# Shared-expert blocks 12 to 15 load turned operands from memory, and the freed tile becomes two more result buffers

## The reference

```python
x = x + 0.5 * ffn(layernorm(x))      # called "a" below
x = x + mamba(layernorm(x))          # "m"; adds its own input as a residual too
x = x + 0.5 * ffn(layernorm(x))      # "b"

def ffn(flat):                       # flat: 4096 x 512
    scores, topk_idx = softmax(flat @ router_w.T), top_k(flat @ router_w.T + router_bias, 4)
    # each of 64 experts takes the first 64 tokens that chose it (its slots)
    xg = flat[tok_table]                                    # 64 x 64 x 512
    y = down(silu(gate(xg)) * up(xg)) * weight              # width 128 per expert
    out = zeros.at[tok_table].add(y)
    return out + sh_down(silu(sh_gate(flat)) * sh_up(flat)) # shared experts, width 1024 in all
```

## Time and profile before

| | us |
|---|---|
| time, median of 3 runs | 2304.61 |
| lowest and highest run | 2303.82 to 2307.62 |
| profiled execution, its own time | 2305.35 |
| its span, first to last instruction | 2303.6 |
| PE busy in the span | 2252.9 (98%) |
| DVE, ACT, POOL busy | 1363.3, 882.4, 693.7 |

### The profile page before, as it was taken

One profiled execution on the slowest core, in us unless ns is written; L12 is line 12 of the kernel. 1 busy time (PEld: TensorE's weight loads), 2 busy tenths in 40 slices (PEclk: granted clock), 3 DMA queues, 4 the chain that ended last, 5 costly groups with the idle time before them and its releaser, 6 DMA issues.

```text
span 2303.6 us, 41271 instructions
## 1 busy us (share of the span) xinstructions
PE 2252.9 (98%) x16412; PEld 2003.2 (87%) x16412; DVE 1363.3 (59%) x3201; ACT 882.4 (38%) x1563; POOL 693.7 (30%) x534
## 2 busy tenths in 40 slices
PE   6999999999998999999999999999999999999998
PEld 6999998777798899999998999998999999777787
DVE  6777762222228677777777777778777763223322
ACT  5232321233327555554555555455323231223321
POOL 1244443112220433233332223331144444122222
PEclk9999999999999999999999999999999999999999
DMA  8776525989844111111111111104376532988949
GB/s 273 263 260 209 164 84 181 306 282 284 236 89 138 45 30 36 28 28 29 28 28 29 28 28 29 28 22 169 125 282 224 199 104 78 312 291 286 290 83 183
DMA packets 129279, 334.73 MB, mean 145 GB/s; under 512 B 24450, under 2 KB 45186, under 8 KB 118400
## 3 DMA queue, kind: packets, MB, share of 16 engines
q1 hardware_dynamic: 80592, 236.63, 28.7%
q0 software_dynamic: 48496, 95.46, 18.1%
HBM read 218.25 MB, written 172.77 MB: 170 GB/s over the span
## 4 chain that ended last, share of the span: by engine, by line
PE 87%; DVE 4%; ACT 4%; DMA 3%; issue 1%; SPq 0%; DVEq 0%; POOL 0%; ACTq 0%; POOLq 0%
PE m_p_ab L1687 3%; PE m_p_x L1687 3%; PE m_p_x L1689 3%; PE m_p_x L1688 3%; PE m_p_ab L1689 3%; PE m_p_ab L1688 3%; PE p_up_b L769 3%; PE p_x_b L873 3%; PE p_x_a L873 3%; PE p_up_a L769 3%; PE p_gate_b L769 2%; PE m_p_y L1808 2%; PE m_p_y L1809 2%; PE p_up_b L771 2%; PE p_up_b L770 2%; PE p_gate_b L770 2%
## 5 line engine op out<-in xcount | busy, mean ns | idle before, releaser
L2004 DVE SCALAR_TENSOR_TENSOR m_xt<-m_ssm,m_convw,m_xt 128x256 f32<-128x256 f32 x384 | 211.9, 565 | 55.2 <-ACT m_ssm L1553 46.0
L1687 PE MATMUL m_p_ab<-m_ht_hi,m_wi_b_hi 128*128 128x256 f32 x576 | 164.5, 286 | 3.8 <-ACT m_ssm L1553 3.4
L506 POOL DMA_INDIRECT slot_rows<-a_hr,a_slot_now x128 | 128.4, 1003 | 131.3 <-PE p_gate_a L771 81.0
L506 POOL DMA_INDIRECT slot_rows<-b_hr,b_slot_now x128 | 128.9, 1007 | 129.5 <-PE p_gate_b L771 80.1
L1688 PE MATMUL m_p_ab<-m_ht_lo,m_wi_b_hi 128*128 128x256 f32 x576 | 161.3, 280 | 0.0
L1689 PE MATMUL m_p_ab<-m_ht_hi,m_wi_b_lo 128*128 128x256 f32 x576 | 161.2, 280 | 0.0
L769 PE MATMUL p_gate_a<-a_hts_hi,a_w_hi 128*128 128x256 f32 x512 | 148.4, 290 | 1.8 <-DVE a_hts_lo L1068 1.8
L1457 POOL TENSOR_TENSOR m_state_dec<-m_state,m_etot 128x1024 f32<-128x1024 f32 x31 | 74.0, 2386 | 248.7 <-ACT m_etot L1569 248.7
L769 PE MATMUL p_gate_b<-b_hts_hi,b_w_hi 128*128 128x256 f32 x512 | 147.0, 287 | 0.3 <-DVE b_hts_lo L1068 0.3
L769 PE MATMUL p_up_a<-a_hts_hi,a_w_hi 128*128 128x256 f32 x512 | 145.5, 284 | 0.0
L769 PE MATMUL p_up_b<-b_hts_hi,b_w_hi 128*128 128x256 f32 x512 | 145.4, 284 | 0.0
(11 more groups left out here) (378 smaller groups left out, 7346.7 us busy)
## 6 DMA issues: line engine op xcount, KB each, us to landing
a_ew<-in_ew SPq DMA_DIRECT2D x32, 1536.0 KB, 7.2
b_ew<-in_ew SPq DMA_DIRECT2D x32, 1536.0 KB, 7.3
after_ffn<-a_zeros POOLq DMA_DIRECT2D x6, 2048.0 KB, 9.2
out<-b_zeros POOLq DMA_DIRECT2D x6, 2048.0 KB, 10.1
slot_rows<-a_zeros POOLq DMA_DIRECT2D x1, 8336.0 KB, 37.1
a_rows<-slot_rows SPq DMA_DIRECT2D x32, 260.5 KB, 8.4
b_rows<-slot_rows SPq DMA_DIRECT2D x32, 260.5 KB, 8.2
m_x<-after_ffn SPq DMA_DIRECT2D x16, 512.0 KB, 3.6
```

The lines of the kernel that those rows point to most:

```text
L506: g_.indirect_dma_start(out=xg, out_offset=bass.IndirectOffsetOnAxis(ap=slot_now[r % HR][:, at:at + 1], axis=0), in_=hr[r % HR][:, j, :], ...
L1687: t.matmul(out, l_hi, r_hi_, start=first, stop=False)
L2004: ins_ = v.scalar_tensor_tensor(xt[:, m, :], ssm[:, m, i:i + BM], convw[:, m, i:i + 1], xt[:, m, :], ALU.mult, ALU.add)
```

## The change

`FROM_MEMORY` grows to blocks 2 to 15, and with it the code that it steers: rounds 6 and 7 are stored too (16 more stores of 256 KB per FFN), blocks 12 to 15 are loaded (8 more loads of 512 KB per FFN), and `normed`, `turn_s` and `turned_s` run for blocks 0 and 1 alone. The tile `hs` [128, 2, 512] is then free when the routed experts begin; its two halves become the sixth and seventh `y` buffer, so ACT waits for the add of pair `q - 7`. POOL's wait ahead of the read for block 15 is now for the load of those rows. Two waits follow from the same table: ACT waits for stores of `turned_rows` in rounds 6 and 7 before it reuses `htr_hi` (L661), and the fill of the Mamba tile that lies where `hs` was waits for four groups of transposes and no longer for twelve (L1409).

```diff
-EY = 5
+EY = 5 + TS
-FROM_MEMORY = range(2, 12)
+FROM_MEMORY = range(2, NS)
...
-        y = [ex(f"y{u}", [P, D]) for u in range(EY)]
+        y = [ex(f"y{u}", [P, D])[:] for u in range(EY - TS)] + [hs[:, j, :] for j in range(TS)]
...
-                    in_=y[q % EY][:], in_offset=None, bounds_check=2 * HALF - 1, oob_is_err=True,
+                    in_=y[q % EY], in_offset=None, bounds_check=2 * HALF - 1, oob_is_err=True,
...
-                pool.wait_ge(hs_mid, own(NS - 1) * TS)
+                pool.wait_ge(late_loaded, 16 * (NS - LATE))
...
-                a.activation(y[q % EY][:], p_x2[:], ACT.Copy).then_inc(y_ready, 1)
+                a.activation(y[q % EY], p_x2[:], ACT.Copy).then_inc(y_ready, 1)
```

## The result

The change made the kernel slower. Its median is 2316.86 us (six runs, 2315.30 to 2325.72), that of the kernel before, with three more runs beside it, 2305.62; the ratio is 1.0054, with a 95% interval of 1.0038 to 1.0070. The profiled execution took 2316.88 us, its span is 2315.2. The prediction was 2304.1, with a range up to 2309.0: the sign and the size are both wrong.

A forecast was written before the change was run, and what follows sets the result against it. PE was taken to bound the kernel, with POOL's chain of adds 1.1 us behind it at b's end; a's -3.8 and b's +3.3 gave -0.5 us, so 2304.1 us against 2304.61, range 2299.2 to 2309.0.

The forecast's parts named there:

- b's part of the sum, +3.3: In FFN b POOL's chain ends last: -1.1 + 0.2 + 4.2 = +3.3 us, hiding PE's earlier end.
- four loads then lengthen the chain by 4.2 us: POOL's chain of adds: four 1 MB loads at 1.06 us per MB add 4.2 us; high bound 10.4.
- a's part: FFN a: PE's net saving of 3.8 us shows fully, since Mamba's start can follow PE.
- PE's saving: Each FFN: eight transpose groups at 0.44 us plus 0.5 at two block ends, 4.0 us saved.
- rival 3: Loads push pairs' weights back on SP's queue and PE waits: 22 us lost, 2326 us; chance 0.05.
- Rival 4: A transpose on PE is worth 0.275 us, so a gains 5.3 us more: 2298.8 us; chance 0.02.
- This chain ends only 1.1 us ahead of PE's: End of b: POOL's last add lands at 2298.1, PE's chain with its store ends at 2299.2.
- The estimate from that page's fit: POOL's adds: at 2.4 us per 1 MB load, losing all of it four times makes 9.6 us.
- Merges at no cost: End of b: the sum held no added time for the merges behind the last pair's add.
- Which covers 4.4 + 4.2: ACT's waits for adds: two more buffers give some 11 us, covering the longest wait 4.4 plus chain growth 4.2.
- Stores: Rounds 6 and 7: two more stored rounds cost PE 0 to 0.6 us, taken as 0.2 per FFN.
- Rival 2: Every load costs what block 11's did, 2.6 us; POOL's chain grows by 10.4: 2310.3 us; chance 0.13.

The follow-up runs named there:

- after, again: The changed kernel, unaltered, measured a second time against the kernel before: 2319.37 us against 2305.47, ratio 1.0066.
- half of the bytes: Changed kernel with loads for blocks 12 to 15 bringing only the hi half, against the kernel before: 2302.86 us against 2307.31, ratio 0.9986.
- with 14's load behind, again: Change in FFN a alone, block 14's load behind the last pair's loads, repeated against the kernel before: 2305.38 us, ratio 0.9994.

## Why the prediction was wrong

The step that failed is b's part of the sum, +3.3, and in it the term "four loads then lengthen the chain by 4.2 us". The mechanism was right: the loads slow POOL's adds, and POOL's chain ends b. But with the change in b alone the time rose by 14.8 us, and without the loads there by 0.5; in the profiles the chain grew by 7.0 to 9.7, and points 2 and 4 add 2.6 that the sum left out. a's part held by the runs, -5.1 and -3.2 with the change in a alone against the forecast -3.8, though single executions stall (point 5).

The profiled executions, by the prediction's own terms (us against the kernel before; the first row is the issue of b's first add, and the rows add up to the span):

| term | predicted | after | after, again |
|---|---|---|---|
| a and Mamba, up to b's first add | -3.8 + 0.2 | +3.0 | -2.8 |
| b's chain of pair adds | +4.2 | +7.0 | +7.0 |
| block 13's add to block 14's | 0 | +1.5 | +1.5 |
| POOL's lead over PE | -1.1 | 0 | 0 |
| sum | -0.5 | +11.6 | +5.8 |

1. **PE's saving: right.** 4.0 us from each FFN. a's block 12 went from 61.72 to 60.84 us, block 14 from 34.57 to 33.49; PE never waited for `hts`, and rival 3 is out. Rival 4 is out with it: four transposes were worth 0.44.

2. **"This chain ends only 1.1 us ahead of PE's": wrong, worth 1.1 us of the sum.** I compared when two transfers landed. POOL's add landed at 2298.07 and SP's store at 2299.37 in the trace, and I took the later one for the end. But the store waits among POOL's merges: in seven profiles its second half was issued from 0.34 us ahead of the last merge's landing to 1.08 behind it, and landed 1.27 to 1.30 us behind block 14's add each time. And the program doesn't end with it: the span ends 5.53 us behind the add in these seven, and 5.53 or 5.54 in the nine where the store landed 0.3 to 2.8 us ahead of the add. SP's waits at the end, before (first fence) and after:

```profile
SPq L2190 <- PEq L2190: 2.5, 1, 2.5
SPq L485 <- DMA out<-b_xs: 2.4, 1, 2.4
...
SPq L2190 <- DMA out<-b_xs: 1.3, 1, 1.3
```

```profile
SPq L485 <- DMA out<-b_xs: 15.0, 1, 15.0
SPq L2190 <- PEq L2190: 3.8, 1, 3.8
```

   The 2.4 and the 15.0 end when block 14's add lands (2298.07 and 2309.6). From there SP waits 1.3 us for the store and 2.5 more for PE's queue in the kernel before; after the change the store has landed earlier, and the wait for PE's queue alone is 3.8, the same sum. In the one profile whose store came late (5.9 us behind the add, the change in a alone, again), the span ended 1.89 us behind it; so the store of before had at least 5.53 - 1.30 - 1.89 = 2.3 us to spare. POOL's chain already ended the program.

3. **The loads' price in b, 4.2 us: too small.** It was 7.0 in both profiles of the changed kernel and 9.7 with the change in b alone. I spread the loss of the stage evenly over the bytes on SP's queue (1.06 us per MB) and weighed the one add beside block 11's load lightly. The profiles show no even price. From the issue of pair 0's add to that of pair 8's, from there to pair 16's, and to pair 24's, b took 76.6, 69.1 and 68.7 us before, and after the change 75.7, 78.3 and 70.0 (75.8, 78.2 and 70.0 in its second profile). The middle lot took 76.0 to 78.3 in the four profiles with the whole load for block 12 in it, and 68.6 to 76.6, median 71.2, in the eleven without: that load costs most, the later ones less. The trace of before alone did not tell it: its first lot, with block 11's load, is 7.5 us longer than the next, which four times would be 30. The DMA engines were at a share of 0.91 in block 11 of b before and of 0.94 after (286 and 303 GB/s), so little was free; half of the bytes hid almost wholly, the whole did not. The Trainium skill (DMA: Bandwidth & Descriptors, Queues, rings and completion order) has the engines take turns between queues. The trace agrees in direction: the add beside block 12's load took 9.6 us. The estimate from that page's fit, 9.6 us for the four loads, lies 2.6 above the 7.0, mine 2.8 below.

4. **Merges at no cost: wrong by 1.5.** With POOL late and PE early, block 15's stores run among the merges (3.9 us against 11.4). From the landing of the last pair's add to that of block 14's it took 52.0 to 53.7 us in the eight profiles with late stores and 53.5 to 55.2 in the nine with early ones. Two of the nine have no loads for blocks 12 to 15 at b's end, so it isn't the loads; that it is the stores was not tried by itself.

5. **"Which covers 4.4 + 4.2": wrong in a.** Two more buffers gave 11 us by my estimate; a's chain fell behind by up to 18.7 us at pair 20 in the first profile. ACT waited 8.55 us, PE lost 4.04 and then ran at a granted clock of 0.57. Rivals and sum had no term for it, since I took a's chain to have 28 us until Mamba and looked at its end alone. It does not come each time: two of the four profiles of a with whole loads show it (53.82, 53.44), two don't (48.08). (With block 14's load behind the pairs it was 48.08 twice, 50.09 and 50.35.) With the stall a's block 15 starts 1.2 us later than before (684.49 against 683.27), without it 3.4 earlier (679.87): the stall takes a's saving. The code of before can stall in the same way: with b unchanged, two profiles (the change in a alone, again, and with 14's load behind, again) have some 9.5 us more in b's block 12. The first of them shows there:

```profile
ACT b_y L693 <- DMA out<-b_y,b_row_no: 18.7, 3, 11.2
```

```profile
2176.28 3.68 PE L876 MATMUL p_x_b<-b_ew,b_xt 128*64 128x256 f32 x16 [7.18 <-DVE b_pt L1114]
```

   ACT waited 11.2 us for one add, PE 7.18: five buffers, no new loads. Such stalls in single executions may be why medians of the same kernel differ by 2 to 3 us; that was not shown.

6. **Stores: right, and small.** Blocks 6 and 7 of both FFNs took 38.4 us before and after.

Rival 2 (the price of block 11's load, 2.6 us each) came nearest: its 10.4 for b's chain lies above the 7.0 to 9.7 of the profiles, and its 2310.3 is still too low, since it lacked points 2, 4 and 5.

What stays open: from the start of a's block 15 to b's first gate product, which is Mamba in the main, it took 901.2 us in the profile before and 904.9 in the one after, which is part of the +3.0. It is not the change's (900.4 in its second profile, and 900.1 to 905.5 over all), but what makes it vary isn't known. And the runs put b's loads at about 14 us (b alone +14.8, without the loads +0.5), while the profiles account for 8 to 10 of it (b's chain 280.3 with them, 272.3 without, 270.6 before): the rest may be stalls in runs that were not profiled, which was not shown.

## What to carry to other kernels

Ask which chain the last wait needs, not which transfer lands last: here a store landed 1.3 us behind an add because it waited among the transfers ahead of that add, and ended nothing. A serial chain of transfers that is never idle pays for traffic put beside it (here 7 to 10 us for 4 MB), and work taken off an engine that runs beside it gains nothing where the chain ends the stage; move such work only in the part where the other engine ends it (here FFN a). Spare time on a shared resource need not be proportional: half of each load was nearly hidden, the whole one was not.

## What the hardware showed that was not expected

An add of 256 KB that took 4.8 us where no weights are loaded took 9 to 11 us beside one 1 MB load and a pair's weights (9.6 in b, 11.1 in a). In a the wait for the late add left PE idle for 4.04 us, which was followed by a stretch of 4 us at a granted clock of 0.57, near the lower level of 1.2 GHz, after PE had been busy for 4.96 of 9 us; a's block 13 was 5.7 us longer in all.
